# Four attention units in a row, then a step, the weighted sum and a second step, in the first layer of a two-layer transformer

## The reference

```python
xn = _layernorm(x, axis=-1)
s = _L0_attn_ref(xn, ...)      # two attentions of 8 heads on the halves of xn, one on a
                               # smoothed copy (holt), then a 128-512-128 feed-forward
g = _silu(_L0_ffn_ref(xn, ...))
x = x + s * g
xn = _layernorm(x, axis=-1)
s = _L1_attn_ref(xn, ...)      # 16 heads of width 8, causal, with alibi
g = _silu(_L1_ffn_ref(xn, ...))
return x + s * g

def mha(xin, ...):             # layer 0; the causal one of layer 1 is alike
    scores = jnp.einsum('bshd,bthd->bhst', q, k) * (1.0 / np.sqrt(DK))
    a = jax.nn.softmax(scores, axis=-1)
    o = jnp.einsum('bhst,bthd->bshd', a, v).reshape(b, s, DH)
    return o @ wo.T + bo
```

## Time and profile before

| | |
|---|---|
| time, median of 3 runs | 1276.57 us (1275.53 to 1281.41) |
| profiled execution, own time | 1285.47 us |
| its span | 1283.5 us |
| PE busy | 1049.2 us, 82% |
| DVE busy | 776.5 us, 60% |
| ACT busy | 656.6 us, 51% |
| POOL busy | 541.2 us, 42% |
| mean granted TensorE clock | 0.926 of full speed |
| chain that ended last: PE, POOL, DVE | 51%, 18%, 9% |

### The profile page before, as it was taken

One profiled execution on the slowest core, in us unless ns is written; L12 is line 12 of the kernel. 1 busy time (PEld: TensorE's weight loads), 2 busy tenths in 40 slices (PEclk: granted clock), 3 DMA queues, 4 the chain that ended last, 5 costly groups with the idle time before them and its releaser, 6 DMA issues.

```text
span 1283.5 us, 24573 instructions
## 1 busy us (share of the span) xinstructions
PE 1049.2 (82%) x8630; PEld 544.6 (42%) x8630; DVE 776.5 (60%) x1696; ACT 656.6 (51%) x1245; POOL 541.2 (42%) x568
## 2 busy tenths in 40 slices
PE   5349889969989898988899787784699978889982
PEld 5112249623333333333334444342589944434541
DVE  6359772457878787878755646754244446557710
ACT  1000662446767666667666545353244446556672
POOL 3154400062727272737363724477100056654344
PEclk9955999989999999999999989797799989899997
DMA  6345347661414141414141415244488843433211
GB/s 180 118 124 127 85 131 211 209 148 34 105 29 106 29 103 34 108 26 116 27 117 27 117 26 151 68 123 136 115 243 249 239 121 89 111 82 87 60 35 41
DMA packets 133348, 137.60 MB, mean 107 GB/s; under 512 B 14233, under 2 KB 115193, under 8 KB 133017
## 3 DMA queue, kind: packets, MB, share of 16 engines
q1 hardware_dynamic: 127096, 123.59, 37.1%
q0 software_dynamic: 6144, 12.60, 3.8%
HBM read 88.11 MB, written 54.58 MB: 111 GB/s over the span
## 4 chain that ended last, share of the span: by engine, by line
PE 51%; POOL 18%; DVE 9%; issue 6%; ACT 6%; DMA 4%; SPq 1%; POOLq 0%; ACTq 0%; DVEq 0%
PE ps_banks L526 7%; PE ps_banks L491 5%; PE ps_banks L1422 5%; PE ps_banks L483 5%; POOL sent L1552 5%; POOL tokens L868 4%; DVE a_neg_max L727 4%; PE ps_banks L602 3%; PE ps_banks L1435 2%; PE ps_banks L1217 2%; PE ps_banks L1203 2%; PE ps_banks L597 2%; PE ps_banks L545 2%; PE ps_banks L502 2%; PE ps_banks L566 2%
## 5 line engine op out<-in xcount | busy, mean ns | idle before, releaser
L727 DVE TENSOR_REDUCE a_neg_max<-ps_banks 128x1 f32<-128x512 f32 x512 | 325.8, 684 | 95.2 <-PE ps_banks L491 93.3
L642 ACT ACTIVATE a_probs<-ps_banks 128x512 f32<-128x512 f32 x512 | 282.9, 598 | 142.8 <-PE ps_banks L483 140.5
L491 PE MATMUL ps_banks<-k_strip,q_strip 51*128 51x128 bf16 (+2 forms) x1536 | 299.0, 296 | 42.9 <-DMA k_strip<-k_rows 21.6
L483 PE MATMUL ps_banks<-q_strip,k_strip 53*128 53x128 bf16 (+3 forms) x1408 | 283.7, 299 | 16.8 <-DVE a_neg_max L727 6.8
L644 ACT ACTIVATE a_probs<-ps_banks 128x512 f32<-128x512 f32 x256 | 146.9, 598 | 113.6 <-PE ps_banks L483 111.0
L491 PEld LDWEIGHTS ps_banks<-k_strip,q_strip 51*128 51x128 bf16 x1536 | 101.3, 95 | 233.9 <-ACT a_probs L642 109.7
L868 POOL DMA_INDIRECT tokens<-made,at x96 | 92.9, 968 | 155.5 <-DMA made<-work 127.9
L483 PEld LDWEIGHTS ps_banks<-q_strip,k_strip 53*128 53x128 bf16 x1408 | 94.8, 95 | 123.2 <-ACT a_probs L642 52.6
L729 DVE TENSOR_REDUCE a_neg_block<-ps_banks 128x4 f32<-128x512 f32 x128 | 87.2, 689 | 95.9 <-PE ps_banks L491 94.7
L526 PE MATMUL ps_banks<-a_probs,v_aug 128*32 128x512 f32 x1024 | 140.4, 621 | 0.0
L732 DVE TENSOR_REDUCE a_neg_block<-ps_banks 128x4 f32<-128x512 f32 x128 | 83.2, 683 | 31.8 <-PE ps_banks L491 31.5
(11 more groups left out here) (223 smaller groups left out, 1691.1 us busy)
## 6 DMA issues: line engine op xcount, KB each, us to landing
work<-in_pack SPq DMA_DIRECT2D x40, 450.0 KB, 3.5
q_rows<-a_q_parts SPq DMA_DIRECT2D x96, 128.0 KB
k_rows<-a_k_parts SPq DMA_DIRECT2D x96, 128.0 KB
q_strip<-q_rows SPq DMA_DIRECT2D x64, 192.0 KB
k_strip<-k_rows SPq DMA_DIRECT2D x64, 192.0 KB
work<-in_w SPq DMA_DIRECT2D x32, 256.0 KB, 3.2
sent<-in_zeros SPq DMA_DIRECT2D x14, 512.0 KB, 7.9
work<-sent SPq DMA_DIRECT2D x56, 128.0 KB, 3.2
```

The costliest lines, as they stand in the source:

```text
L483: mm = pe.matmul(sbank[:, at:at + hi - lo], k_now[rows(js, ROW_END), slot, kt * P:(kt + 1) * P], q_now[rows(js, ROW_END), slot, lo:hi], st ...
L491: mm = pe.matmul(mbank[:, at:at + hi - lo], q_next[rows(jm, ROW_SHIFT), slot, qt * P:(qt + 1) * P], k_next[rows(jm, ROW_SHIFT), slot, lo:h ...
L642: act.activation(probs[si // 4 % 2][:, si % 4, :], bank, ACT.Exp).then_inc(sems["probs"], 1)
L727: dve.tensor_reduce(neg_max[:, half, hd, qt:qt + 1], bank, AX.X, ALU.max, negate=True).then_inc(sems["max_out"], 1)
```

## The change

In layer-0 stages the places come in pairs after every fourth unit. The sum of a group is one unit later, after unit 4g+7 (`LATE[0]` = 4), and stands between the two places of the pair: four units, a step, the sum, a second step. The wait inside the sum step is counted one unit further back to fit. In stage 8, whose leftover layer-0 steps run in a layer-1 rhythm, "norm" of the last quad and "onT" are two places and one place later (`LAST0`). The code that puts the first place ahead of the sum holds for layer 1 too: where a place and a sum fall on one unit, the step now stands before the sum. The steps, units and their data are the same.

```diff
+LATE = (QT, 3)
...
+LAST0 = {**MISC[0], 2: [], 4: [("norm", -1, QT - 1)], 5: [], 6: [("onT", -1)]}
...
     def misc(place):
         for k in range(2):
-            for step in MISC[k].get(place, []):
+            for step in (LAST0 if b == NB and k == 0 else MISC[k]).get(place, []):
...
-        late = {at + RING - last: (-1, g) for at, g in sums_of(layer(-1)).items() if at + RING >= last}
+        late = {at + LATE[layer(-1)] - last: (-1, g) for at, g in sums_of(layer(-1)).items() if at + LATE[layer(-1)] >= last}
     if live(0):
-        late.update({at + RING: (0, g) for at, g in sums_of(layer(0)).items()})
+        late.update({at + LATE[layer(0)]: (0, g) for at, g in sums_of(layer(0)).items()})
...
+        due = place
+        while due < PLACES and (due + 1) * units <= (u + 1) * PLACES:
+            due += 1
+        if units == UNITS[0]:
+            due = due // 2 * 2
+        if place < due:
+            misc(place)
+            place += 1
         if scores and u in late:
-            total(*late[u], RING)
-        while place < PLACES and (place + 1) * units <= (u + 1) * PLACES:
+            total(*late[u], LATE[layer(late[u][0])])
+        while place < due:
             misc(place)
             place += 1
```

## The result

The change makes the kernel slower. The median of four runs is 1317.91 us (1315.51 to 1321.37), beside 1278.99 us (1275.53 to 1282.14) of the kernel before on the same chip: a ratio of 1.0307, 95% interval 1.0267 to 1.0347. The forecast was 1320 us with a chance of 0.92 for slower. The profiled execution took 1321.37 us, its span 1319.5 us, against 1285.47 and 1283.5 before. Its mean granted clock is 0.918 (0.926 before).

What follows compares the result with a forecast made beforehand. PE was taken as the bound, DVE close behind. Five full stages at 6.5 us more (32.5) plus partial stages made 40 us, the clock 4: 1276.6 + 44 = 1320 us, range 1297 to 1338.

Steps and rivals of the forecast that it cites:

- the rival that DVE sets the pace: Also called "faster": in full stages only the order of PE's waits changes; stage 62.4 us, whole 1260 us; chance 5%.
- The fourth unit, nothing or ACT's reader ahead: Layer-0 groups: fourth unit starts 1.2 (nothing ahead) or 1.28 us after the first, waiting 0.54 or 0.61 us.
- Behind "proj" and "ff2": Two groups a stage: fourth unit starts 3.28 and 2.84 us after the first, waiting 2.6 and 2.2 us.
- 15.8 us of waits at fourth units: Full layer-0 stage: total wait of PE before the fourth units of 16 groups, 2.4 + 4.7 + 2.6 + 2.2 + 3.9 us.
- the groups of "minus" and "mix": Groups of units 0, 32 and 60, with that DVE work ahead: 1.5, 0.95 and 1.45 us, together 3.9.
- A stage of 71.2 us at full clock: Full layer-0 stage: work 51.9, block ends 1.6, fourth-unit waits 15.8, remaining waits 1.9 us; 64.7 before.
- Waits for the misc bank mostly gone: Layer-0 stages: most waits of steps for their bank's reader vanish; about 1.9 us stay, "norm" behind ACT's "take" included.
- Stages 2 to 6: Five full layer-0 stages: 6.5 us more each, 32.5 us in all, before the clock's 4 us.
- Stage 0: Only 1 us more: largely at low clock without the previous batch's steps, units take twice as long, DVE keeps up.
- Stage 7: 40 maxima for 64 units, so only the exponential's part of the fourth unit's wait: 2.5 us more.
- The clock: Layer-0 stages: one more dip in each of five, among long waits behind "proj" and "ff2"; 4 us in all.
- The rival of a clock that falls in many more groups: Dips of 0.8 us behind every wait above 0.9, four more a stage: 22 us, whole 1338 us; chance 10%.

Runs made afterwards that it cites:

- e4: Layer-0 maxima over 256 of 512 columns, in both kernels: before 1263.38 us (ratio 0.9885), changed 1286.17 (1.0048), both ratios against the unhalved kernel before.
- e3: Changed kernel with "proj" moved ahead of "k", and "ff2a", "ff2" ahead of "shift"; ratio to the kernel before 1.0123, on a second chip 1.0166.
- e0: The changed kernel run once more, unaltered: 1314.45 us against 1280.46 of the kernel before on the same chip, ratio 1.0261.
- e1: Kernel before with only the sum one unit later, places behind every second unit as before; ratio to the kernel before 1.0129, on a second chip 1.0123.
- e2: Kernel before with places in pairs behind every fourth unit, sum still behind the third; ratio to the kernel before 1.0206, on a second chip 1.0225.
- e8: Kernel before with "ff2a" and "ff2" one place later: 1277.08 us against 1280.46 of the kernel before, ratio 0.9981.

## Why the prediction held, point by point

- **PE leads, and three banks let it run three units ahead.** Held. PE's busy time in a stage is nearly unchanged and idle time makes the difference; DVE gets idler (9.8 to 16.9 us before the maxima), so the rival that DVE sets the pace falls. e4 says the same: halving the maxima gave 17 us of the kernel before and took 11 of the change's 34.
- **The fourth unit, nothing or ACT's reader ahead.** Forecast 1.2 to 1.28 us from first to fourth unit, measured 1.29 in the group above.
- **Behind "proj" and "ff2".** Forecast 3.28 and 2.84 us, measured 3.34 and 2.84. e3 shows their weight: with both covered, a stage is some 3.4 us shorter, one dip of the clock included.
- **15.8 us of waits at fourth units.** Measured 14.9. In the stage from 394.0 us the sixteen groups need 1.30 us nine times, 1.34 twice, then 1.52, 1.68 twice, 2.84 and 3.34, together 25.4, less 16 x 0.66. The shown 11.3 us are less, since shown idle time begins at the end of a matmul row. The term was too large in the groups of "minus" and "mix": 1.0, 0.6 and 1.0 us, where 1.5, 0.95 and 1.45 were forecast.
- **A stage of 71.2 us at full clock.** None of the full stages ran at full clock. The measured 71.7 less two dips of 1.1 us (e0) would be 69.5, an estimate, so the sum is about 1.7 too large. Of that 0.9 is the fourth units' and 1.5 the misc bank's (next point); 51.9 + 1.6 + 14.9 + 0.4 makes 68.8, so some 0.7 us stand in the stage that the terms don't name.
- **Waits for the misc bank mostly gone.** Held: 0.4 us in the stage, before "proj" and "shift", where I had allowed 1.9. "yT" has none.
- **Stages 2 to 6.** Forecast 32.5 and 4 more for the clock, 36.5; measured 32.7.
- **Stage 1.** Forecast 4, measured 5.3. The granted clock was 0.87 there, 0.91 before.
- **Stage 0.** Forecast 1, measured 0.2, and the reason given was wrong. The low clock belongs to the stretch ahead of it, with maxima alone (0.53 from 66 to 128.5 us); from 134.5 to 180 us it is 1.00 in both kernels. There the fourth units do wait, fifteen times and 7.2 us in all, but the kernel before waited 6.0 us in the same 45.5, in other places, 2.8 of it for DVE, which was busy for 39.4. So in this stretch the waits only moved, which is what the rival "faster" had said of the full stages.
- **Stage 7.** Forecast 2.5, measured 0.3. The fourth units wait 2.8 us as shown, eight times and at most 0.4. What the other groups gained for it was not taken apart.
- **Layer 1.** Forecast 0; the lag falls by 2.5 us there. e7, with that side of the change alone, shows no gain (interval -0.35 to +0.13%, within which a gain of 2.5 us, 0.2%, still lies). It stays open whether this is a later start of the layer or the scatter of single executions.
- **The clock.** The number of dips was right, their price (0.8) a little low, and the places were not all right. I expected dips behind "proj" and behind "ff2" (unit 51). The stretches of the stage at 400 us show one behind "proj", another some 10 us later, and none behind unit 51, where there was one before:

```profile
416.00:420.00 4.00, 4.00 (x21) 1.94 (x20) 1.50 (x3) 1.19 (x2) 3.31 (x3) 0.61 0.62 169
428.00:432.00 4.00, 3.95 (x26) 0.76 (x19) 2.79 (x5) 2.07 (x4) 1.54 (x2) 0.68 0.02 6
455.00:459.00 4.00, 3.51 (x26) 1.22 (x30) 3.87 (x7) 2.73 (x6) 3.89 (x5) 1.00 0.00 0
```

- **The rival of a clock that falls in many more groups.** Of the 4-us stretches of that stage four are below 1.00, the two above and two at the edges of these dips, at 0.96 and 0.89; the mean clock of a stage is 0.95 where this rival needed five dips. The rule behind it (the Trainium skill, TensorE: Matmul & The Clock Gate, A second HAM failure mode: psum-queue depth-cycling) describes gaps like these sixteen. The trace agrees behind "proj" and shows thirteen gaps of 0.4 to 0.8 us, most of which the clock passes at full speed.
- **The whole.** The terms made 44 us, the spans of the two profiled executions differ by 36.0 and the medians by 38.9. By part: stages 0 and 1, 5 forecast and 5.5 measured; stages 2 to 6, 36.5 and 32.7; stage 7 and layer 1, 2.5 and -2.2. So the loss was put some 5 to 8 us too high. That the time of 1317.9 lies within 2.1 of the forecast 1320 is in part luck: the forecast stood on 1276.6 us for the kernel before, which measured 1279.0 beside the changed one, and the medians lie 3 us further apart than the traces.

## What to carry to other kernels

With the ring of three banks here, the fourth unit of an unbroken row waits for the first unit's readers. Where the issuing engine sets the pace, as in the full stages, that wait is lost time; in stage 0, where DVE was as busy as PE (39.4 and 39.5 of 45.5 us before), it only took the place of others. Put other work of the issuing engine between unit n and unit n+1 of a ring of n banks, as long as the reader's latency less the row's own time (here 1.29 - 0.66 = 0.63 us, against a sum of 0.99). Grouping like work saves only the seams, 0.10 us each here; it takes away the filling that hid the ring, and what two neighbours hid from each other appears as a wait in a third place, as e1 and e2 show. The step whose reader holds the consumer longest goes to the front of the filling, not to its end: in e3 that gave back about half of the loss.

## What the runs showed of the hardware that I had not expected

- The granted clock does not follow the length of a single wait. In the changed kernel it is 0.61 behind a wait of 2.51 us and 1.00 behind one of 2.01 us in the same stage. In the order of before it is 0.62 behind a wait of 1.01 us and behind one of 1.24 us (e8), but the stage from 450.3 us has waits of 1.02 and 1.26 us and a clock of 1.00 throughout.
- Taking away the wait ahead of a dip need not take away the dip: in two of e8's five full stages it came behind the next wait instead, and in e3, without waits above 0.8 us at fourth units, four of five full stages still had one.
- Half the columns in the maxima made the start of the fourth unit only 0.16 us earlier (1.30 to 1.14, behind "logits"). The exponential of the other bank begins 0.48 us after the unit and takes 0.59, so it ends at nearly the same time as a whole maximum, which begins 0.46 us after the unit and takes 0.65.
